# A four-layer graph kernel: T's row sums asked for one stage later, and layer 3's first group put through layer 2's pipeline

## The chip, the core and the metric

The kernel runs on one core of a Trainium2 chip. The metric is the device time of one launch in microseconds (us); less is better. The engines are TensorE (PE in the rows; its weight loads are PEld), VectorE (DVE), ScalarE (ACT), GpSimd (POOL) and SyncE (SP), which issues all DMAs. Each engine works through its own queue in order and waits at semaphores. Semaphores count up; `wait_ge(sem, n)` holds the queue until the count is n.

## What is computed

There are 128 graphs of 64 nodes with 512 features. Each of four layers adds an attention-like term to x. Cut to the parts that matter here:

```python
def gnn3(X, A):                                   # layer 3
    Xw = X @ Wv + bv
    sj, si = Xw @ aw[:d, 0], Xw @ aw[d:, 0]
    e = leaky_relu(sj[:, None, :] + si[:, :, None] + ab[0], 0.2)
    alpha = A * exp(e)
    T = alpha / (sum(alpha, axis=-1) + 1e-12)
    H, Xk = 0, X
    for k in range(3):
        H = H + Xk @ Wk[k] + bk[k]
        Xk = T @ Xk
    return relu(H)

# each layer, 0 to 3
h = maximum(layernorm(x), 0.0)
x = x + gnn_layer(h, adj)
```

Layer 2 is multi-head attention with 8 heads of 64, whose scores are multiplied by twice the adjacency ahead of the softmax, with projections q, k, v and o.

## The kernel before

All 8192 tokens are cut into 16 groups (`NG`) of 512 tokens, and each group into 4 tiles of 128 tokens (two graphs). A float32 product is made of three passes over values split in two parts, `hi` and `lo`: ScalarE copies the `hi` part and VectorE or GpSimd subtracts to get `lo`. Each engine's queue is written out by hand, one function for each (`pe_program`, `dve_program`, `act_program`, `pool_program`, `sp_program`), with the layers' loops over groups in it. Nothing reorders them.

Results of TensorE lie in 8 banks, taken in turn; each waits for the eviction of what lay there eight takes before. `bank.done(key)` is the wait for a bank's result.

The way of a group's input: SyncE loads x; VectorE makes statistics (`stats_A`, L629 and L631); GpSimd makes the scale (`scale_A`, L1188 to L1193); ScalarE normalizes into `hn` (`norm_A`, L961); VectorE transposes blocks into `hs` (`transposes`, L650); SyncE gathers `hs` into `hGA` with 16 DMAs (`gather`, L1392); ScalarE and another engine split this into `hi` and `lo` (`features2_hi`, L947, and `features_lo`, L1201).

Layer 2, group g. TensorE: q projection, first half of the context of group g-1 (`l2_ctx`), k projection, output tile 0 of g-1 (`l2_out`), second half of the context, output tiles 1 to 3 with the scores between, v projection, and the transposes of the probabilities P (`l2_pT`). ScalarE evicts these into `ptc` (L1139), and VectorE evicts v into `VV` (L877); the next context needs both. A further pass of the loop, g = NG, does what remains of the last group.

Layer 3, group g. TensorE makes z2 = h W2 in four tiles; then four tiles of z1 = h W1, each with the product of T and z2 added by three matmuls (a "hop", `l3_hop`, L589); then four tiles of y = h W0, each with the hop of T and z1. The hops need `T`'s parts (count `v_tlo`) and z's (`Z0`, `Z1`).

T of a group comes about like this. VectorE makes the sums `scol` over `hn` (`l3_sums`, L935, L940). SyncE writes one column to DRAM (L1425), waits, and reads it back spread over all partitions as `si` (L1429; `rows3`). VectorE adds and takes the leaky relu (`l3_alpha`, L817, L821), ScalarE the exponential (L1099), GpSimd multiplies with the adjacency, giving `al` (L1312). TensorE sums rows of `al` with a matrix of ones (`l3_rowsum`, L583). VectorE takes the reciprocal (L888, L890), GpSimd multiplies (`tt`, L1319), ScalarE and VectorE split the product into `T` (`Thi`, `Tlo`).

Before, all this for group g+1 is asked for within group g: the row-sum matmul stands behind y tile 1 of group g on TensorE, and the rest of T behind it on the others. And layer 3's group 0 has its own places in the last passes of layer 2: its statistics, norm and transposes stand between and behind the last group's softmax, and its weights `W3[2]` are split in the extra pass.

Of the kernel before, what the change touches and what calls it, by code (L numbers as in the profile page):

```python
# [74 lines left out]
def build(nc, x, adj, nodemask, L0_gnn_Wqk, L0_gnn_Wv, L1_gnn_Wq_w, L1_gnn_Wq_b, L1_gnn_Wk_w, L1_gnn_Wk_b,  # L75
# [12 lines left out]
    with root:  # L88
# [183 lines left out]
        def pe_program(eng):  # L272
# [266 lines left out]
            for g in range(NG + 1):  # L539
# [22 lines left out]
                for u in range(2):  # L562
# [3 lines left out]
                    if on:  # L566
                        l2_scores(g, u)
                if on:
# [7 lines left out]
            def l3_rowsum(g):  # L576
                if g >= NG:
                    return
# [13 lines left out]
            for g in range(NG):  # L592
# [14 lines left out]
                for t in range(4):  # L607
                    b, full, _ = gemm_open(("y", g, t), hT3[i], t, W3[0], (v_y, 4 * g + t + 1), False)
                    l3_hop(b, full, g, t, 1)
                    if t == 1:  # L610
                        l3_rowsum(g + 1)


        def dve_program(eng):
# [208 lines left out]
            for g in range(NG + 1):  # L823
# [6 lines left out]
                if g + 1 < NG:  # L830
                    stats_A(2, g + 1)
                if g == NG - 1:
                    dve.wait_ge(d_vec3, 64)
                    for k in range(4):
                        eng.scalar_tensor_tensor(sc3[:], wv3[:, k, :], 1.0, awb[:, 0, :], ALU.mult, ALU.mult,
                                                 accum_out=af[:, k, 0:1]).then_inc(v_af, 1)
                        dve.wait_ge(v_af, k + 1)
                if prev:
                    l2_out(g - 1, 0)
                if g + 1 < NG:  # L840
                    transposes(2, g + 1)
# [4 lines left out]
                if g == NG - 1:  # L846
                    for k in range(4):
                        eng.scalar_tensor_tensor(sc3[:], wv3[:, k, :], 1.0, awb[:, 1, :], ALU.mult, ALU.mult,
                                                 accum_out=af[:, k, 1:2]).then_inc(v_af, 1)
                        dve.wait_ge(v_af, k + 5)  # L850
# [3 lines left out]
                for u in range(2):  # L854
# [5 lines left out]
                    if u == 0 and g == NG - 1:  # L860
                        stats_A(3, 0)
                if g == NG - 1:
                    transposes(3, 0)
                    m = dve.step(eng.tensor_tensor(sc3[:], awb[:, 0, :], awb[:, 1, :], ALU.add))
                    dve.wait_ge(s_dve, m)
                    m = dve.step(eng.scalar_tensor_tensor(sc3[:], sc3[:], 1.0, bvb[:], ALU.mult, ALU.mult, accum_out=cst))
                    dve.wait_ge(s_dve, m)
                    eng.tensor_tensor(cst, cst, abc, ALU.add).then_inc(v_cst, 1)
# [13 lines left out]
            def l3_rowsum(g):  # L882
                if g >= NG:
                    return
# [5 lines left out]
                eng.reciprocal(rs[:], rs[:]).then_inc(v_rs, 1)  # L890
                dve.wait_ge(a_thi, 2 * g + 2)
# [7 lines left out]
            for g in range(NG):  # L899
                if g + 1 < NG:  # L900
                    stats_A(3, g + 1)
                for t in range(4):
                    l3_zlo(0, ("z2", g, t), g, t)
                    if g == 0 and t == 0:
                        l3_rowsum(0)
# [7 lines left out]
                l3_alpha(g + 1)  # L913
                xt = xs[x_slot(kA(3, g))]
                for t in range(4):
# [6 lines left out]
                    if t == 1:  # L922
                        l3_rowsum(g + 1)
# [19 lines left out]
        def act_program(eng):  # L943
# [157 lines left out]
            for g in range(NG + 1):  # L1101
# [11 lines left out]
                if g + 1 < NG:  # L1113
                    norm_A(2, g + 1)
# [9 lines left out]
                if g == NG - 1:  # L1124
                    norm_A(3, 0)
                if on:
                    l2_exp(g, 1)
                else:
                    split_in_place(W3[1], d_w1)
                if g + 1 < NG:  # L1130
                    act.wait_ge(*bank.done(("v2", g - 1, 3) if g else ("v1", NG - 1, 3)))
                    features2_hi(2, g + 1, hT2[(g + 1) % 2])
# [452 lines left out]
```

## Time and profile before

| | us |
|---|---|
| median of 3 runs | 2554.03 (2552.31 to 2554.06) |
| the profiled execution | 2550.87 |
| its span, first to last instruction | 2549.1 |
| TensorE busy, by the page | 2379.6 (93% of the span) |
| VectorE busy | 1357.8 (53%) |
| ScalarE busy | 818.2 (32%) |
| GpSimd busy | 816.5 (32%) |
| mean granted clock of TensorE | 0.968 of full speed |

The profile's page holds the busy time of each engine, the span cut into 40 slices, and the costliest groups of instructions. Behind it lie views that can be asked for: the timeline of one engine, who waited for whom, the DMA issues, and sums over stretches. A gap in square brackets is the idle time of the engine before the row, with what ended it. The layers take up, one after another, roughly 1200 us for layers 0 and 1, to 1730 us for layer 2, and the rest for layer 3. Instructions are pipelined, so on TensorE a row's start minus the start of the row before is its cost.

### The profile page before, as it was taken

The numbers are of one execution on the slowest core, as the hardware profiler recorded it, in microseconds if no ns is written. First come the engines' busy times: TensorE is split into PE (matmuls) and PEld (weight loads), VectorE is DVE, ScalarE is ACT, GpSimd is POOL, SyncE is SP. The second block draws the span as 40 slices with busy tenths as digits, with TensorE's granted clock in tenths as the row PEclk, the third lists the DMA queues.
The fourth block names the chain that finished last, engine by engine and source line by source line (L and its number), as shares of the span: only waits on it lengthen the run. The fifth ranks groups of instructions, "written<-read, shape, count | busy, mean of one in ns | idle before, by whom it ended". The sixth has DMA issues, their size and how long they took to land.

```text
span 2549.1 us, 39522 instructions
## 1 busy us (share of the span) xinstructions
PE 2379.6 (93%) x15951; PEld 1935.6 (76%) x15951; DVE 1357.8 (53%) x2570; ACT 818.2 (32%) x1493; POOL 816.5 (32%) x1015
## 2 busy tenths in 40 slices
PE   8899999999999999999999999997788878878887
PEld 4688888888888887888888888886677667766766
DVE  2565556656565545445444544556555555555553
ACT  2343334334343433333333333333112212221220
POOL 2354545545455333233223322325111111111120
PEclk9999999999999999999999999999899989988999
DMA  5223332233323432112212221234222223222320
GB/s 161 71 71 88 107 80 78 75 92 99 84 74 80 128 108 81 55 55 80 84 55 57 82 79 55 60 93 142 60 79 77 64 60 91 73 60 61 92 52 37
DMA packets 164007, 202.70 MB, mean 80 GB/s; under 512 B 71712, under 2 KB 71792, under 8 KB 163824
## 3 DMA queue, kind: packets, MB, share of 16 engines
q1 hardware_dynamic: 163824, 200.18, 27.8%
q8 instruction: 125, 2.05, 0.4%
q14 instruction: 58, 0.48, 0.1%
HBM read 82.62 MB, written 50.37 MB: 52 GB/s over the span
## 4 chain that ended last, share of the span: by engine, by line
PE 71%; issue 9%; SPq 6%; DVE 6%; ACT 3%; DMA 2%; POOL 2%; ACTq 0%; DVEq 0%; POOLq 0%
PE bank L313 32%; PE bank L303 27%; SPq L1392 6%; PE bank L329 2%; PE bank L375 2%; DVE hs L650 2%; ACT hn L961 1%; DVE stA L629 1%; PE bank L522 1%; ACT Z_hi L947 1%; PE bank L495 1%; DMA hGA<-hs 1%; PE bank L293 1%; PE bank L589 1%; PE bank L505 1%
## 5 line engine op out<-in xcount | busy, mean ns | idle before, releaser
L313 PE MATMUL bank<-w_hi,h3T_hi 128*128 128x512 f32 x768 | 317.6, 414 | 0.0
L313 PE MATMUL bank<-w_lo,h3T_hi 128*128 128x512 f32 x768 | 309.5, 403 | 0.0
L313 PE MATMUL bank<-w_hi,h3T_lo 128*128 128x512 f32 x768 | 308.4, 402 | 0.0
L961 ACT ACTIVATE hn<-x,stA 128x512 f32<-128x512 f32 x192 | 140.7, 805 | 168.8 <-POOL stA L1193 167.7
L313 PEld LDWEIGHTS bank<-w_hi,h3T_hi 128*128 128x128 f32 x768 | 152.1, 198 | 32.8
L313 PEld LDWEIGHTS bank<-w_lo,h3T_hi 128*128 128x128 f32 x768 | 151.4, 197 | 32.7
L313 PEld LDWEIGHTS bank<-w_hi,h3T_lo 128*128 128x128 f32 x768 | 150.6, 196 | 33.1
L1188 POOL TENSOR_SCALAR stA<-stA 128x4 f32<-128x4 f32 x48 | 11.6, 241 | 512.0 <-DVE stA L631 511.8
L618 DVE TENSOR_TENSOR Z_lo<-bank,Z_hi 128x512 fp32r<-128x512 f32 x128 | 81.4, 685 | 172.4 <-ACT Z_hi L947 172.4
L650 DVE STREAM_TRANSPOSE hs<-hn 128x512 f32<-128x512 f32 x192 | 123.7, 688 | 73.6 <-ACT hn L961 73.6
L1201 POOL TENSOR_TENSOR h3T_lo<-hGA,h3T_hi 128x512 fp32r<-128x512 f32 x64 | 84.5, 1322 | 228.8 <-ACT h3T_hi L947 228.8
L618 DVE TENSOR_TENSOR cT_lo<-bank,cT_hi 128x256 fp32r<-128x256 f32 x128 | 44.8, 410 | 205.2 <-ACT cT_hi L947 205.2
L629 DVE BATCH_NORM_STATS2 stA<-x 128x6 f32<-128x512 f32 x192 | 128.0, 666 | 7.4 <-DMA x<-in_x 7.4
L583 PE MATMUL bank<-alt,bones 128*128 128x256 f32 x32 | 19.0, 697 | 117.4 <-POOL alt L1312 117.4
L1239 POOL TENSOR_TENSOR vv_lo<-vf,vv_hi 128x512 fp32r<-128x512 f32 x64 | 82.6, 1290 | 115.7 <-ACT vv_hi L947 115.7
L303 PE MATMUL bank<-h0T_hi,m_hi 128*128 128x512 f32 x256 | 101.5, 397 | 14.4 <-POOL h0T_lo L1201 14.4
L1201 POOL TENSOR_TENSOR h0T_lo<-hGA,h0T_hi 128x512 fp32r<-128x512 f32 x64 | 99.7, 1588 | 38.9 <-ACT h0T_hi L947 38.9
L790 DVE TENSOR_TENSOR x<-bank,x 128x512 f32<-128x512 f32 x64 | 41.8, 675 | 131.2 <-PE bank L313 122.2
L1272 POOL TENSOR_TENSOR x<-x,abf 128x512 f32<-128x512 f32 x64 | 80.6, 1296 | 79.1 <-ACT hn L961 79.1
L313 PE MATMUL bank<-v_hi,h0T_hi 128*128 128x512 f32 x256 | 104.7, 409 | 0.0
L1260 POOL TENSOR_TENSOR zt<-zt,sm 128x512 f32<-128x512 f32 x64 | 66.9, 1045 | 116.7 <-DVE sm L804 116.7
L313 PE MATMUL bank<-o2w_hi,cT_hi 128*128 128x512 f32 x256 | 103.7, 405 | 0.6 <-DVE cT_lo L618 0.6
(235 smaller groups left out, 6204.0 us busy)
## 6 DMA issues: line engine op xcount, KB each, us to landing
hGA<-hs SPq DMA_DIRECT2D x768, 64.0 KB, 2.0
mid<-x SPq DMA_DIRECT2D x32, 1024.0 KB, 4.7
x<-mid SPq DMA_DIRECT2D x32, 1024.0 KB, 5.8
x<-in_x SPq DMA_DIRECT2D x16, 1024.0 KB, 6.0
hGB<-hs SPq DMA_DIRECT2D x256, 64.0 KB, 2.0
out<-x SPq DMA_DIRECT2D x16, 1024.0 KB, 4.9
abf<-in_adj SPq DMA_DIRECT2D x64, 64.0 KB, 5.0
adj<-in_adj SPq DMA_DIRECT2D x64, 64.0 KB, 3.4
```

Source lines behind the costliest of these rows:

```text
L303: ins = eng.matmul(b[:], W[l][:, k, os], h[r][:, k, :], start=(k == 0 and i == 0), stop=(k == 3 and i == 2))
L313: ins = eng.matmul(b[:], h[l][:, k, ts], W[r][:, k, :], start=(k == 0 and i == 0), stop=(last and k == 3 and i == 2))
L329: ins = eng.matmul(b[h, t * 64:(t + 1) * 64], left[:, k, ts], right[:, 2 * i:2 * i + 2, 4 * k + t, :], start=(k == 0), stop=(k == 3))
L618: return eng.tensor_tensor(lo, src, hi.bitcast(F), ALU.subtract)
L629: m = dve.step(eng.bn_stats(st[:, t, 0:6], xt[:, t, :]))
L650: eng.transpose(hs[:, :, :, t, :].rearrange("p b c r -> p c b r"), (hn1 if layer == 1 else hn)[t][:].rearrange("p (c b r) -> p c b r", c=4 ...
L961: eng.activation(h[t][:], xt[:, t, :], ACT.Relu, bias=st[:, t, 10:11], scale=st[:, t, 9:10]).then_inc(done, 1)
L1201: eng.tensor_tensor(by_token(h["lo"], q), hG[:, q], by_token(h["hi"], q).bitcast(F), ALU.subtract).then_inc(done, 1)
L1239: eng.tensor_tensor(vv["lo"][:, t, :], vf[t % 2][:], vv["hi"][:, t, :].bitcast(F), ALU.subtract).then_inc(p_vlo, 1)
L1260: eng.tensor_tensor(z3, z3, s8(sm[r][:, 0:8]), ALU.subtract).then_inc(p_sb, 1)
L1272: eng.tensor_tensor(xt[:, t, :], xt[:, t, :], bo2[:], ALU.add).then_inc(p_xb, 1)
L1392: eng.dma_start(hG[b * 32:b * 32 + 32, q].rearrange("p c r -> p (c r)"), hs[q * 32:q * 32 + 32, b].rearrange("p c t r -> p (c t r)")).then ...
```

## The change

No instruction's work is changed and none is added or left out of the computation; waits and places in the queues are.

In layer 3, `l3_rowsum(g)` moves from group g-1's y tile 1 to behind the first z2 tile of group g itself, on all engines. On VectorE it is cut in two: the reciprocal goes behind the first Z0 eviction and the split of T (`l3_tlo`) behind the second. `l3_alpha(g+1)` moves on VectorE from ahead of the y evictions to behind y tile 1.

Between layers 2 and 3, a helper `after2(g)` names the group that follows group g of layer 2: (2, g+1), or (3, 0) behind the last. Statistics, scale, norm, transposes and gather of (3, 0) take the place in the loop that such steps of a next group always have. The preparatory sums (`af`, `cst`), the zeroing of `abf`, and the split of `W3[2]` move with them. SyncE gathers ahead of loading `W3[2]` and `W3[1]`, which change places. The adjacency transpose of group 0 moves one output tile back on TensorE. In the diff below, the pieces up to line 610 are of TensorE, those from 827 to 922 of VectorE, from 1104 to 1171 of ScalarE, at 1328 of GpSimd and at 1508 of SyncE.

```diff
+        def after2(g):
+            return (2, g + 1) if g + 1 < NG else (3, 0)
...
@@ -553,7 +557,6 @@
                     l2_out(g - 1, 0)
-                    l3_adj(0)
...
+                    elif u == 0:
+                        l3_adj(0)
...
@@ -595,8 +598,8 @@
-                    if g == 0 and t == 0:
-                        l3_rowsum(0)
+                    if t == 0:
+                        l3_rowsum(g)
...
-                    if t == 1:
-                        l3_rowsum(g + 1)
...
@@ -827,27 +828,28 @@
-                if g + 1 < NG:
-                    stats_A(2, g + 1)
+                if on:
+                    stats_A(*after2(g))
                 if g == NG - 1:
                     dve.wait_ge(d_vec3, 64)
-                    for k in range(4):
...
+                    for h in range(2):
+                        for k in range(4):
...
+                    m = dve.step(eng.tensor_tensor(sc3[:], awb[:, 0, :], awb[:, 1, :], ALU.add))
...
+                if on:
+                    transposes(*after2(g))
...
-                    if u == 0 and g == NG - 1:
-                        stats_A(3, 0)
-                if g == NG - 1:
-                    transposes(3, 0)
...
@@ -901,8 +894,10 @@
+                    if t == 0:
+                        l3_rowsum(g)
+                    if t == 1:
+                        l3_tlo(g)
...
-                l3_alpha(g + 1)
                 xt = xs[x_slot(kA(3, g))]
...
                     if t == 1:
-                        l3_rowsum(g + 1)
+                        l3_alpha(g + 1)
...
@@ -1104,14 +1098,10 @@
-                if not on:
-                    split_in_place(W3[2], d_w2)
-                    act.wait_ge(v_cst, 1)
-                    features2_hi(3, 0, hT3[0])
...
+                elif on:
+                    act.wait_ge(v_cst, 1)
+                    features2_hi(3, 0, hT3[0])
+                    split_in_place(W3[2], d_w2)
...
@@ -1161,8 +1152,8 @@
+                    if t == 1:
+                        l3_thi(g)
...
-                l3_thi(g + 1)
...
@@ -1328,12 +1313,13 @@
+                if g:
+                    if g + 1 < NG:
+                        scale_A(3, g + 1)
+                    l3_rowsum(g)
...
-                l3_rowsum(g + 1)
...
@@ -1508,7 +1493,12 @@
-                gather(2, g + 1)
+                if on:
+                    gather(*after2(g))
+                if g == NG - 1:
+                    sp.wait_ge(*bank.done(("k2", g, 3)))
+                    eng.dma_start(W3[2]["raw"][:], rows(L3_gnn_Wk[2])).then_inc(d_w2, 16)
+                    eng.dma_start(W3[1]["raw"][:], rows(L3_gnn_Wk[1])).then_inc(d_w1, 16)
```

VectorE in layer 3, before, from the second y eviction of a group to the transposes for the next (`rst` the row sums, `yt` the y evictions, `BN_STATS` the statistics):

```order
L921 SCALAR_TENSOR_TENSOR x<-yt,x 128x512
L888 TENSOR_SCALAR rst<-bank 128x256
L890 RECIPROCAL rst<-rst 128x256
L618 TENSOR_TENSOR Tlo<-ttt,Thi 64x4x64 x2
L919 TENSOR_TENSOR yt<-bank,bsumt 128x512
L921 SCALAR_TENSOR_TENSOR x<-yt,x 128x512
L919 TENSOR_TENSOR yt<-bank,bsumt 128x512
L921 SCALAR_TENSOR_TENSOR x<-yt,x 128x512
L629 BN_STATS stA<-x 128x6
...
L618 TENSOR_TENSOR Z_lo<-bank,Z_hi 128x512 x2
L650 STREAM_TRANSPOSE hs<-hn 128x4x4x32 x4
```

VectorE in layer 3 with the change, from the end of alpha:

```order
L822 SCALAR_TENSOR_TENSOR ec<-zct 128x256
L913 TENSOR_TENSOR yt<-bank,bsumt 128x512
L915 SCALAR_TENSOR_TENSOR x<-yt,x 128x512
L913 TENSOR_TENSOR yt<-bank,bsumt 128x512
L915 SCALAR_TENSOR_TENSOR x<-yt,x 128x512
L630 BN_STATS stA<-x 128x6
...
L619 TENSOR_TENSOR Z_lo<-bank,Z_hi 128x512
L879 TENSOR_SCALAR rst<-bank 128x256
L881 RECIPROCAL rst<-rst 128x256
L619 TENSOR_TENSOR Z_lo<-bank,Z_hi 128x512
L619 TENSOR_TENSOR Tlo<-ttt,Thi 64x4x64 x2
L651 STREAM_TRANSPOSE hs<-hn 128x4x4x32 x4
```

The reciprocal and T's split have left the middle of the y evictions and stand between the Z evictions, behind the statistics; alpha (`zct`, `ec`) has gone into the y evictions.

ScalarE from layer 2 to layer 3, before (`zt` the exponentials of the softmax, `hn` the norm, `ptc` the transposed probabilities, `w_hi` the weights of layer 3, `cT_hi` the context):

```order
L1091 ACTIVATE zt<-zt 128x512 x2
L961 ACTIVATE hn<-x,stA 128x512 x4
L1091 ACTIVATE zt<-zt 128x512 x2
L947 ACTIVATE ptc<-bank 128x512 x4
L947 ACTIVATE cT_hi<-bank 128x4x64 x4
L947 ACTIVATE w_hi<-w_raw 128x512 x4
L947 ACTIVATE h3T_hi<-hGA 128x16x32 x4
L947 ACTIVATE cT_hi<-bank 128x4x64 x4
```

ScalarE there with the change:

```order
L1085 ACTIVATE zt<-zt 128x512 x4
L941 ACTIVATE h3T_hi<-hGA 128x16x32 x4
L941 ACTIVATE w_hi<-w_raw 128x512 x4
L941 ACTIVATE ptc<-bank 128x512 x4
L941 ACTIVATE cT_hi<-bank 128x4x64 x8
L941 ACTIVATE atc<-bank 64x256 x2
L1093 ACTIVATE ec<-ec 128x256
```

The norm of layer 3's group 0 has moved from between the exponentials to ahead of the context, and the `h3T_hi` and `w_hi` copies have moved from behind the context's first half to ahead of the `ptc` copies.

## Rows read from the trace of the kernel before

**Rows 1.** The page of the profile, its first line.
```profile
span 2549.1 us, 39522 instructions
```

**Rows 2.** Waits, 1769 to 2468 us: who <- for whom: us, times, longest.
```profile
PE bank L583 <- POOL alt L1312: 109.1, 14, 8.3
...
DVE yt L919 <- PE bank L589: 24.4, 17, 2.0
```

**Rows 3.** Timeline, TensorE: start us, us, line, tiles [idle before <-releaser].
```profile
1995.05 1.22 PE L583 MATMUL bank<-alt,bones 128*128 128x256 f32 x2 [7.93 <-POOL alt L1312]
...
2031.60 0.50 PE L589 MATMUL bank<-Z_hi,Thi 128*128 128x512 f32 x1
...
2504.55 0.39 PE L313 MATMUL bank<-w_hi,h3T_hi 128*128 128x512 f32 x1
...
2542.40 0.39 PE L589 MATMUL bank<-Z_hi,Tlo 128*128 128x512 f32 x1
```

**Rows 4.** Timeline row of TensorE, then busy times and granted clock of a stretch.
```profile
1783.10 0.79 PE L589 MATMUL bank<-Z_hi,Thi 128*128 128x512 f32 x1 [2.17 <-DVE Z_lo L618]
...
1783.07:1786.48 3.41, 3.38 (x8) 2.71 (x9) 1.76 (x3) 1.33 (x4) 0.11 (x1) 0.50 0.00 0
```

**Rows 5.** Timeline, SyncE's DMA issues in layer 3.
```profile
1769.00 3.10 SPq L1392 DMA_DIRECT2D hGA<-hs  x5
...
1969.31 10.06 SPq L1392 DMA_DIRECT2D hGA<-hs  x16
...
1987.82 0.34 SPq L1429 DMA_DIRECT2D sirows<-si  x1
...
2018.21 10.06 SPq L1392 DMA_DIRECT2D hGA<-hs  x16
...
2467.79 10.94 SPq L1392 DMA_DIRECT2D hGA<-hs  x16
```

**Rows 6.** Timeline, VectorE, one turn of layer 3.
```profile
1992.41 0.87 DVE L817 TENSOR_TENSOR zct<-sirows,stB 64x256 f32<-64x256 f32 x2 [7.97 <-DMA sirows<-si]
...
1996.79 0.42 DVE L888 TENSOR_SCALAR rst<-bank 128x256 f32<-128x256 f32 x1
...
2000.73 0.87 DVE L618 TENSOR_TENSOR Tlo<-ttt,Thi 64x256 fp32r<-64x256 f32 x2 [1.74 <-ACT Thi L947]
...
2005.40 0.69 DVE L629 BATCH_NORM_STATS2 stA<-x 128x6 f32<-128x512 f32 x1
...
2014.45 1.29 DVE L618 TENSOR_TENSOR Z_lo<-bank,Z_hi 128x512 fp32r<-128x512 f32 x2 [5.76 <-ACT Z_hi L947]
...
2015.65 2.48 DVE L650 STREAM_TRANSPOSE hs<-hn 128x512 f32<-128x512 f32 x4
```

**Rows 7.** Timeline, TensorE, from layer 2 to layer 3.
```profile
1731.56 3.69 PE L522 MATMUL bank<-ptc,VV 64*64 64x64 f32 x128 [6.99 <-DVE VV L877]
...
1742.26 1.11 PE L338 MATMUL bank<-ident,abf 128*128 128x128 f32 x4 [3.43 <-DMA abf<-in_adj]
...
1752.44 0.39 PE L313 MATMUL bank<-w_hi,h3T_hi 128*128 128x512 f32 x1
```

**Rows 8.** Timeline, VectorE's first reduction of L835, then SyncE.
```profile
1687.97 0.68 DVE L835 SCALAR_TENSOR_TENSOR sc<-wv,awb 128x512 f32<-128x512 f32 x1
...
1705.88 0.93 SPq L1504 DMA_DIRECT2D arows<-stB  x2
...
1714.52 0.33 SPq L1506 DMA_DIRECT2D arowt<-arows  x1
```

**Rows 9.** Timeline, ScalarE, from layer 2 to layer 3.
```profile
1723.20 2.07 ACT L947 ACTIVATE ptc<-bank 128x512 f32<-128x512 f32 x4 [1.97 <-PE bank L505]
...
1734.72 2.21 ACT L947 ACTIVATE w_hi<-w_raw 128x512 fp32r<-128x512 f32 x4
```

**Rows 10.** DMA issues near 1716.7 and 1735.7: KB each, us to landing.
```profile
w_raw<-in_L_gnn_Wk SPq DMA_DIRECT2D x1, 1024.0 KB, 9.0
...
w_raw<-in_L_gnn_Wk SPq DMA_DIRECT2D x1, 1024.0 KB, 5.9
```

More of the change, by code:

```diff
@@ L829, in dve_program @@
                     l01_x2(NG - 1, range(4))
-                if g + 1 < NG:
-                    stats_A(2, g + 1)
+                if on:
+                    stats_A(*after2(g))
                 if g == NG - 1:
                     dve.wait_ge(d_vec3, 64)
-                    for k in range(4):
-                        eng.scalar_tensor_tensor(sc3[:], wv3[:, k, :], 1.0, awb[:, 0, :], ALU.mult, ALU.mult,
-                                                 accum_out=af[:, k, 0:1]).then_inc(v_af, 1)
-                        dve.wait_ge(v_af, k + 1)
+                    for h in range(2):
+                        for k in range(4):
+                            eng.scalar_tensor_tensor(sc3[:], wv3[:, k, :], 1.0, awb[:, h, :], ALU.mult, ALU.mult,
+                                                     accum_out=af[:, k, h:h + 1]).then_inc(v_af, 1)
+                            dve.wait_ge(v_af, 4 * h + k + 1)
+                    m = dve.step(eng.tensor_tensor(sc3[:], awb[:, 0, :], awb[:, 1, :], ALU.add))
+                    dve.wait_ge(s_dve, m)
+                    m = dve.step(eng.scalar_tensor_tensor(sc3[:], sc3[:], 1.0, bvb[:], ALU.mult, ALU.mult, accum_out=cst))
+                    dve.wait_ge(s_dve, m)
+                    eng.tensor_tensor(cst, cst, abc, ALU.add).then_inc(v_cst, 1)
                 if prev:
                     l2_out(g - 1, 0)
-                if g + 1 < NG:
-                    transposes(2, g + 1)
+                if on:
+                    transposes(*after2(g))
                 if prev:
@@ L1163, in act_program @@
                     l3_zhi(0, ("z2", g, t), g, t)
-                    if g == 0 and t == 1:
-                        l3_thi(0)
+                    if t == 1:
+                        l3_thi(g)
                     if g == 0 and t == 3:
@@ L1276, in pool_program @@
                 on, prev = g < NG, g >= 1
-                if g + 1 < NG:
-                    scale_A(2, g + 1)
-                if g == NG:
-                    pool.wait_ge(v_vv, 4 * NG)
-                    pool.wait_ge(p_xb, 4 * NG)
-                    for tl in abf:
-                        eng.memset(tl[:], 0.0).then_inc(p_abz, 1)
+                if on:
+                    scale_A(*after2(g))
                 l2_residual(g + 1)
@@ L1287, in pool_program @@
                         l2_softmax(g, u)
-                    if u == 0 and g == NG - 1:
-                        scale_A(3, 0)
                 if g == NG - 1:
@@ L1299, in pool_program @@
                             eng.memset(tl[n][:].bitcast(F), 0.0).then_inc(p_zero3, 1)
-                if g == NG:
+                    pool.wait_ge(v_vv, 4 * NG)
+                    pool.wait_ge(p_xb, 4 * NG)
+                    for tl in abf:
+                        eng.memset(tl[:], 0.0).then_inc(p_abz, 1)
+                    features_lo(3, 0, hT3[0], hGA, p_flo3)
                     split_in_place(W3[2], "w2")
-                    features_lo(3, 0, hT3[0], hGA, p_flo3)
             def l3_alpha(g):
@@ L1330, in pool_program @@
             for g in range(NG):
-                if g and g + 1 < NG:
-                    scale_A(3, g + 1)
+                if g:
+                    if g + 1 < NG:
+                        scale_A(3, g + 1)
+                    l3_rowsum(g)
                 if g + 1 < NG:
@@ L1519, in sp_program @@
                 if g == NG - 1:
-                    sp.wait_ge(*bank.done(("qk", g, 2)))
-                    eng.dma_start(W3[1]["raw"][:], rows(L3_gnn_Wk[1])).then_inc(d_w1, 16)
-                    eng.dma_start(W3[2]["raw"][:], rows(L3_gnn_Wk[2])).then_inc(d_w2, 16)
-                    gather(3, 0)
                     sp.wait_ge(*bank.done(("pT", g, 3)))
```

30 lines of the change are left out of this document (5 added, 25 removed).

## The prediction, made before the changed kernel was run

> **What bounds the kernel now.** I read the page first: the span is 2549.1 us [rows 1], TensorE is busy over nine tenths of it, and the digits of the slices fall from 9 to 7 and 8 only in layer 3. So I listed who waits for whom between 1769 and 2468 us. TensorE sat idle 109.1 us, 14 times, before the matmul of L583 that sums T's rows, each time for `al` [rows 2]. VectorE waited 24.4 us for y's banks. TensorE's timeline shows one such wait: idle 7.93 us before 1995.05, then running [rows 3]. The idle costs clock too: a stretch of 3.41 us after a wait of 2.17 us was granted 0.50 [rows 4], which is 1.2 instead of 2.4 GHz.
>
> Why is `al` late? SyncE's queue and VectorE's timeline, read together, give a ring [rows 5, 6]. The gather for group g+1 starts at 1969.31; its 16 issues stand ahead of the store and reload of `si`; the reload is issued at 1987.82, and VectorE takes up the landed rows at 1992.41. Then come two y evictions, the row sums' reciprocal, T, two more y evictions, the next statistics (2005.40), the norm, two Z_lo, the transposes (2015.65), and the next gather (2018.21). Fourteen turns from 1769.00 to 2467.79 make 49.91 us each [rows 5]. A whole group's 168 matmuls in the last group, where nothing waits, take 2504.55 to 2542.79, 38.24 us, or 0.228 us each [rows 3]. **Layer 3 is bound by this ring of latencies, not by TensorE.** What counts is the steps that leave it.
>
> **Part 1, the row sums a stage later.** No work is added or removed. By the new VectorE order, y tiles 0 and 1 are evicted before the alpha step, in the time in which VectorE waited for `si`; tiles 2 and 3 follow alpha.
>
> Walk the new ring with the old durations, from a gather's start. Alpha starts after 23.1 us (1992.41 - 1969.31) [rows 5, 6]. To the statistics: 4.38 us (1996.79 - 1992.41), as before, since alpha and two evictions stand there again, now of tiles 2 and 3. Statistics, GpSimd's scale, ScalarE's norm and Z0_hi: 9.05 us (2014.45 - 2005.40). One Z_lo: 0.6 us (half of 2015.65 - 2014.45). Reciprocal, `tt`, T_hi, T_lo: 4.8 us (1996.79 to 2000.73 and 0.87 more). Transposes to gather: 2.56 us. The new stand of the row sums thus stays in the ring: in ScalarE's order the norm is ahead of Z0_hi, and VectorE takes the sums behind the first Z_lo. What leaves is (a) two evictions, 2.79 us, with the wait for y's banks, 24.4 / 14 = 1.74 us [rows 2], together 4.53 us, the mean from T_lo's end to the statistics; and (b) the second Z_lo, 0.6 us, now hidden under GpSimd's and ScalarE's part of T. The new turn is 49.91 - 5.13 = **44.8 us**. For fourteen turns: **-71.8 us**.
>
> Is `al` in time? It ended about 2.6 us after alpha's start (1995.05 - 1992.41) [rows 3, 6], so 25.7 us after the gather. z2(g+1) starts 24.4 us after the gather: the y0 hop at 13.4 (2031.60 - 2018.21), 0.8 for it, three tiles of 15 matmuls at 3.4. The sum is due 2.7 us after that, at 27.1. It waits for nothing, with 1.4 us to spare.
>
> **What is late next.** TensorE needs T at the first z1 tile, 60 matmuls and the sum after z2's start, 14.1 us. T is ready at 44.8 - 24.4 - 2.6 = 17.8. A new wait of 3.7 us appears at the hop (L589), for T_lo. Behind it in TensorE's queue stands everything; T_hi on ScalarE holds the Z0_hi of tiles 2 and 3 behind it, which TensorE needs 6 us later. The transposes come some 4 us later against z2 than now, so Z1_hi, queued behind the h3T copies on ScalarE, makes the y0 hop wait as well: 31.9 asked, 20.4 + 13.4 = 33.8 ready, 1.9 us. Work 39.1, waits 5.6: again 44.7. Both waits are slack of TensorE, not additions to the ring: y3 is ready at 24.4 and its eviction starts at about 26.
>
> The clock, by rows: half speed for 3.41 us after a wait of 2.17 us [rows 4] loses 1.7 us. After the wait for T this only shortens the second wait. So I take 0, up to +0.6 us a turn (+8) if 10 us at half speed follow it, as y3 would then be 0.6 us late. The Trainium skill, TensorE: Matmul & The Clock Gate, "HAM oscillation — how this bites in real kernels", speaks against the change: short work between waits pays the return to speed at every wait, and two waits now stand where one was. By that rule alone a turn would cost what a second slow stretch costs; the ring's slack hides it by the rows.
>
> **Part 2, the change from layer 2 to 3.** Before, TensorE waits 6.99 us (to 1731.56, for V) and 3.43 us (to 1742.26, for the adjacency of group 0) and starts z2(0) at 1752.44 [rows 7]. V is late since the statistics, the transposes and the work on `cst` of layer 3 stand between and behind layer 2's last softmax on VectorE. They move ahead, into 9 us in which VectorE was idle: 3.3 us of statistics and eight reductions at 0.73 (four start at 1687.97 [rows 8]) end near 1697.2, 8.7 us before the 1705.88 at which SyncE sends their result. Two more operations on `cst` end by 1698.8, before out(14,0) asks at 1699.8. These cost nothing under that cover.
>
> SyncE: everything behind these reductions moves by 8.7 us. The row reload goes from 1714.52 to 1705.8 [rows 8]; the gather of layer 3 follows at once, 16 issues in 10.7 us, to 1716.8; then W3[2] is loaded, now first of the three large transfers. VectorE's V is done near 1723.4, right behind the last v2 tile. **But ScalarE's queue now has W3[2]'s four copies (2.21 us) ahead of the four copies of P^T (2.07 us)** [rows 9], and these wait for the weights. A 1 MB load landed in 9.0 us as first of two behind a store, in 5.9 us alone [rows 10]. I take 5.9, since it has no large transfer ahead of it any more: landed 1722.8, split 1725.0, P^T 1727.1. TensorE resumes at 1727.1 instead of 1731.56, -4.45. With 9.0 us it is 1730.1, -1.4; as the last of three large ones (some 12 us) even +1.5.
>
> The fixed cost and rate in the Trainium skill, DMA: Bandwidth & Descriptors, "Anatomy of one DMA — SWDGE (gpsimd) path", would make it an estimate of 4.4 us; P^T would then wait for TensorE's last transpose instead, and the sum would change by under 1 us.
>
> The 3.43 us go: the zeroing of the diagonal buffers moves behind V on GpSimd, 7 us earlier, and the adjacency transpose moves one output tile back. Alpha(0) gets its `si` some 11 us earlier too (an estimate: V is 7.9 us earlier, and the gather's issues, which hold SyncE's next loads some 4 us beyond the zeroing now, stand ahead of it), and its sum is due only after z2(0)'s first tile, near 1747. Group 0 then runs as now, bound by TensorE to its z2 tiles. Sum of part 2: **-4.45 - 3.43 = -7.9 us**, between -12 and -2.
>
> **The tail.** Now 81.3 us pass from the last gather (2467.79) to the end. Then: 24.4 to z2(15), 38.24 + 0.4 for its matmuls and sum with no wait (no statistics stand ahead of its row sums), 6.3 from the last matmul to the end (2549.1 - 2542.79): 69.4. **-11.9 us.**
>
> **Sum:** -7.9 - 71.8 - 11.9 = -91.6 us. The profiled execution took 2550.87 us, so 2459.3; against the median of 2554.03, 0.1% above it, **2462 us**.
>
> **Rivals.**
> 1. T is in time and TensorE alone bounds layer 3: a turn of 39.1 us, 14 x -10.8 = -151, in all -171, **2383 us**. For it: the waits for `al` are all that TensorE shows now. Against: T's own steps and the 9.05 us of statistics and norm ahead of them are in the rows. 5%.
> 2. The ring is longer than its parts: y3, or the reload of `si`, comes later, because TensorE runs at half speed after both waits (rows of up to 10 us after 8 us of idle exist). With 10.2 and 6.8 us slow, y3 is ready near 31, 4 us late: a turn of about 48.8, **2518 us**; with one of them 2470. 12% beyond 2490.
> 3. W3[2] lands late and P^T with it, the last term from +1.5: about **2468 us**, inside the range. 8%.
> 4. Slower: TensorE does not return to 2.4 GHz between waits 14 and 30 us apart. At half speed throughout, 168 matmuls take 77 us, a turn of 78: +390, **2940 us**. It decides from a turn of 49.91 + (7.9 + 11.9) / 14 = 51.3 us, that is 24 us of each group at half speed; now it is 7 to 10. The skill's clock page reports a clock stuck low for over 50 us, a case of this kind; no row here shows it. 2%.
> 5. The change does not do what it says: `al` is still late and the old wait returns at the new place. The margin is 1.4 us, and reloads vary by 1 us. But a late sum has 9 us until VectorE asks for it, so the turn stays: same time. Held in the forecast.
>
> **Chances.** Forecast 73%, rival 1 5%, 2 12%, 3 8%, 4 2%. The range 2440 to 2490 holds the forecast (turn of 43.5 to 46.5) and rival 3. A measurement of this kernel can tell 0.2%, 5 us, from no change. Faster 96%, the same 1%, slower 3%.
>
> **What would show it.** After: the wait before the row-sum matmul gone; 14 waits of 2 to 4 us of the hop for T_lo, and some of 1 to 2 us for Z1_lo; gathers 44.8 us apart, the first near 1761; P^T's copies starting at 1725 on ScalarE, behind the weights; no wait for the adjacency. Gathers 39 us apart prove rival 1, over 47 rival 2. A first gather later than 1767 makes part 2 wrong.

## The result, and the profile after

The changed kernel took **2462.16 us** (median of 4 runs, 2460.24 to 2465.29), the kernel before 2553.53 us beside it (2552.31 to 2554.06). The ratio is **0.9644**, 95% interval 0.9627 to 0.9661: 3.6% faster. The forecast was 2462 us, faster.

| | before | after | early_sums (below) |
|---|---|---|---|
| span of the profiled execution, us | 2549.1 | 2459.3 | 2379.8 |
| gather for layer 3's group 1 starts at | 1769.00 | 1760.75 | 1762.33 |
| gather for the last group starts at | 2467.79 | 2388.72 | 2306.52 |
| one turn (difference / 14) | 49.91 | 44.86 | 38.87 |
| from the last gather to the end | 81.3 | 70.6 | 73.3 |
| mean granted clock | 0.968 | 0.986 | 0.994 |

Of the 89.8 us by which the span is shorter, 8.25 lie ahead of the first gather, 70.8 in the 14 turns (5.06 each), and 10.7 behind the last gather.

The page's first line and its TensorE line (busy us, share of the span, instructions):

```profile
span 2459.3 us, 39508 instructions
...
PE 2364.3 (96%) x15951; PEld 1923.9 (78%) x15951; DVE 1360.9 (55%) x2570; ACT 820.3 (33%) x1493; POOL 818.1 (33%) x1015
```

Waits of the changed kernel from 1769 to 2389 us (who, for whom: us in total, times, longest), which answer to [rows 2]:

```profile
DVE zct L818 <- DMA sirows<-si: 50.8, 14, 4.2
...
PE bank L592 <- DVE Tlo L619: 43.5, 14, 3.6
DVE yt L913 <- PE bank L592: 22.2, 15, 3.0
...
PE bank L592 <- DVE Z_lo L619: 10.6, 6, 2.3
```

TensorE's 109.1 us for `al` are gone from the list. In their place stand 14 waits for T_lo and 6 for Z_lo, 54.1 us together.

One turn, which answers to [rows 5, 6]. SyncE, with a gather, the reload of `si` and the next gather:

```profile
1806.25 10.28 SPq L1377 DMA_DIRECT2D hGA<-hs  x16
1816.57 0.58 SPq L1410 DMA_DIRECT2D si<-stB  x1
1826.01 0.33 SPq L1414 DMA_DIRECT2D sirows<-si  x1
...
1850.99 10.06 SPq L1377 DMA_DIRECT2D hGA<-hs  x16
```

VectorE in the same turn:

```profile
1829.57 0.87 DVE L818 TENSOR_TENSOR zct<-sirows,stB 64x256 f32<-64x256 f32 x2 [3.86 <-DMA sirows<-si]
...
1833.95 0.69 DVE L630 BATCH_NORM_STATS2 stA<-x 128x6 f32<-128x512 f32 x1
...
1842.99 0.69 DVE L619 TENSOR_TENSOR Z_lo<-bank,Z_hi 128x512 fp32r<-128x512 f32 x1 [5.75 <-ACT Z_hi L941]
1843.60 0.41 DVE L879 TENSOR_SCALAR rst<-bank 128x256 f32<-128x256 f32 x1
...
1848.43 2.49 DVE L651 STREAM_TRANSPOSE hs<-hn 128x512 f32<-128x512 f32 x4
```

And TensorE and GpSimd there: `al`, its row sums, and the hop that waits for T_lo:

```profile
1831.43 0.73 POOL L1298 TENSOR_TENSOR alt<-ec,atc 128x256 f32<-128x256 f32 x1 [11.46 <-ACT ec L1093]
...
1833.62 0.59 PE L586 MATMUL bank<-alt,bones 128*128 128x256 f32 x2
...
1848.45 0.80 PE L592 MATMUL bank<-Z_hi,Thi 128*128 128x512 f32 x1 [3.31 <-DVE Tlo L619]
```

Each step of this turn, with the forecast in brackets: gather to alpha 23.32 us (forecast 23.1), alpha to statistics 4.38 (4.38), to the first Z_lo 9.04 (9.05), the Z_lo 0.61 (0.6), reciprocal to T_lo's end 4.83 (4.8), transposes to the next gather 2.56 (2.56): 44.74 us. `al` ends at 1832.16, 1.46 us before the matmul that needs it (forecast 1.4), and no turn has a wait for it. Only group 0's `al`, in the passage, came 0.57 us late (1747.29).

TensorE from layer 2 to layer 3 in the changed kernel, which answers to [rows 7]:

```profile
1728.91 2.10 PE L526 MATMUL bank<-ptc,VV 64*64 64x64 f32 x128 [2.92 <-ACT ptc L941]
...
1732.34 0.50 PE L317 MATMUL bank<-o2w_hi,cT_hi 128*128 128x512 f32 x1 [1.33 <-DVE cT_lo L619]
...
1737.91 0.60 PE L342 MATMUL bank<-ident,abf 128*128 128x128 f32 x4
...
1743.84 0.39 PE L317 MATMUL bank<-w_hi,h3T_hi 128*128 128x512 f32 x1
```

z2(0) starts 8.60 us earlier (1752.44 to 1743.84), near the 7.9 of the forecast, but by other terms. The next rows show it. They cover both kernels from TensorE's return to z2(0). Each row has the length in us and TensorE's busy time (instructions). Then come the same for the weight loads, VectorE, ScalarE and GpSimd, and the granted clock, the DMA share and GB/s. Of before:

```profile
1731.56:1742.26 10.70, 6.72 (x141) 5.68 (x141) 5.95 (x18) 6.45 (x16) 7.60 (x8) 0.82 0.65 168
1742.26:1752.44 10.18, 10.18 (x41) 8.49 (x41) 0.00 (x0) 0.76 (x2) 3.14 (x3) 0.84 0.12 27
```

Of the changed kernel:

```profile
1728.91:1738.20 9.29, 7.96 (x155) 6.81 (x156) 5.26 (x12) 2.42 (x8) 7.97 (x7) 1.00 0.68 192
1738.20:1743.84 5.64, 5.64 (x27) 4.66 (x26) 0.00 (x0) 0.76 (x2) 0.00 (x0) 1.00 0.21 39
```

TensorE came back 2.65 us earlier, not 4.45. The 3.43 us for the adjacency went, as forecast. A wait for cT_lo (the `lo` part of the context) grew from 0.56 to 1.33 us, which I had not counted; TensorE had run the context ahead of it in 2.10 instead of 3.69 us and so asked sooner. And TensorE was busy 13.60 instead of 16.90 us, since the clock stayed at full speed (1.00) where it had fallen to 0.82 and 0.84: 3.30 us that I had taken as 0. Sum: -2.65 - 3.43 + 0.77 - 3.30 = -8.61.

This sum is of one execution. In another of the same kernel (after_again, below) z2(0) started at 1748.23, 4.4 us later, with a longer wait for cT_lo and the clock at 0.83 from 1725 to 1745 us:

```profile
1733.85 0.80 PE L317 MATMUL bank<-o2w_hi,cT_hi 128*128 128x512 f32 x1 [2.71 <-DVE cT_lo L619]
...
1748.23 0.39 PE L317 MATMUL bank<-w_hi,h3T_hi 128*128 128x512 f32 x1
```

### The profile page after: what moved, and what is told of

Same layout as the page of the kernel before. It is cut to its first block, busy times and chain, and to the rows that moved or that the text cites. A ratio compares the mean times of both kernels' runs of the same rounds, so it can differ in the third digit from the quotient of the medians.

```text
span 2459.3 us, 39508 instructions
## 1 busy us (share of the span) xinstructions
PE 2364.3 (96%) x15951; PEld 1923.9 (78%) x15951; DVE 1360.9 (55%) x2570; ACT 820.3 (33%) x1493; POOL 818.1 (33%) x1015
## 4 chain that ended last, share of the span: by engine, by line
PE 69%; DMA 8%; DVE 8%; SPq 6%; issue 3%; ACT 3%; POOL 2%; ACTq 0%; DVEq 0%; POOLq 0%
PE bank L317 30%; PE bank L307 28%; SPq L1377 6%; DMA si<-stB 5%; PE bank L333 3%; DMA sirows<-si 3%; PE bank L379 2%; DVE hs L651 2%; DVE stA L630 1%; ACT hn L955 1%; PE bank L499 1%; PE bank L526 1%; PE bank L297 1%; DVE rst L881 1%; PE bank L509 1%
## 5 line engine op out<-in xcount | busy, mean ns | idle before, releaser
L317 PE MATMUL bank<-w_hi,h3T_hi 128*128 128x512 f32 x768 | 311.1, 405 | 0.0
L317 PEld LDWEIGHTS bank<-w_hi,h3T_lo 128*128 128x128 f32 x768 | 148.2, 193 | 32.4
L619 DVE TENSOR_TENSOR cT_lo<-bank,cT_hi 128x256 fp32r<-128x256 f32 x128 | 44.8, 411 | 204.0 <-ACT cT_hi L941 204.0
L592 PE MATMUL bank<-Z_hi,Thi 128*128 128x512 f32 x128 | 54.1, 423 | 55.4 <-DVE Tlo L619 43.5
L929 DVE SCALAR_TENSOR_TENSOR yt<-hn,arowt 128x512 f32<-128x512 f32 x128 | 102.1, 852 | 0.0
```

What stands on the lines that cost most here:

```text
L317: ins = eng.matmul(b[:], h[l][:, k, ts], W[r][:, k, :], start=(k == 0 and i == 0), stop=(last and k == 3 and i == 2))
L619: return eng.tensor_tensor(lo, src, hi.bitcast(F), ALU.subtract)
L929: eng.scalar_tensor_tensor(yt[c][:], hn[t][:], 0.0, arow[:, c, :], ALU.max, ALU.mult, accum_out=scol[g % 2][:, t, c:c + 1]).then_inc(v_dot ...
```

## Experiments: the two parts alone

The theory: layer 3 runs at the length of a ring of latencies from gather to gather, part 1 takes 5.1 us out of each turn, part 2 is a one-time gain, and TensorE's new waits are slack. The first rival is that TensorE's waits or its clock set the turn; the second, that the parts' gains are shared out otherwise.

**part1_only**: only layer 3's new places, with the passage as before. Edit against the changed kernel, in short:

```diff
-                if on:
-                    gather(*after2(g))
+                gather(2, g + 1)
...
-                if on:
-                    stats_A(*after2(g))
+                if g + 1 < NG:
+                    stats_A(2, g + 1)
...
```

> Only the layer 3 part of the change: the row sums asked for in the group that needs T, alpha between the y evictions. The passage from layer 2 to 3 is that of the kernel before. Theory (a ring of latencies of 44.8 us a turn, independent of the passage): fourteen turns of 44.8 instead of 49.9 us and a tail 11 us shorter, together about -82 us, 2472 us, ratio 0.968; first gather for group 1 at about 1769 us. Rival (the two parts need each other, since a late group 0 keeps TensorE behind): less than -70 us, with turns above 46 us.

Measured: 2476.3 us (2474.6 to 2479.1), ratio 0.9683 (0.9667 to 0.9699), with the kernel before at 2558.15 us on that chip. Gathers from 1771.37 to 2405.48, a turn of 45.29; 14 waits for T_lo, 52.0 us. Part 1 alone brings 81.9 us.

**part2_only**: only the passage; layer 3's row sums and alpha as before. Edit against the changed kernel:

```diff
-                    if t == 0:
-                        l3_rowsum(g)
+                    if g == 0 and t == 0:
+                        l3_rowsum(0)
...
+                    if t == 1:
+                        l3_rowsum(g + 1)
```

> Only the passage: group 0 of layer 3 goes through layer 2's pipeline, and layer 3's loop is that of the kernel before. Theory: the first gather for group 1 comes 8 us earlier, turns stay at 49.9 us, so about -8 us, 2545 us, ratio 0.9968. Rival (a gain ahead of a loop bound by latencies is taken back by the loop's first wait): within 2 us of the kernel before.

Measured: 2548.16 us (2545.06 to 2549.1), ratio 0.9962 (0.9947 to 0.9977): 10.0 us, a small gain, but clear of the interval. The turn is 50.26 us, with this wait in layer 3 (1762 to 2465 us):

```profile
PE bank L588 <- POOL alt L1304: 113.7, 14, 8.4
```

The parts add up: 81.9 + 10.0 = 91.9 us, where the whole change brought 91.4 and, in after_again, 90.5. The wait for `al` belongs to part 1 and the gain in the passage to part 2.

## Experiments: what sets the turn

**after_again**: the changed kernel, as the base of this set.

> The changed kernel once more, for comparison on this chip: ratio 0.9644 to the kernel before.

Measured: 2467.01 us (2465.35 to 2469.24), ratio 0.9642 (0.9625 to 0.9659), before at 2557.48; a turn of 45.09.

**more_matmul**: the row-sum matmul is done five times, each with the same result: 1.4 us more for TensorE in each group.

```diff
-                eng.matmul(b[:, 0:256], bones[:], ...).then_inc(full, 1)
+                for i in range(5):
+                    ins = eng.matmul(b[:, 0:256], bones[:], ...)
+                ins.then_inc(full, 1)
```

> The changed kernel with the row-sum matmul of each group of layer 3 done five times into the same bank instead of once: four more, at 0.35 us each by the trace, are 1.4 us more work for TensorE in each of 16 groups. Theory (the turn is the ring of latencies, and the wait for T_lo is slack of TensorE): no change, within 4 us of the changed kernel, and the waits for T_lo shrink from about 3.1 to about 1.7 us. Rival (TensorE with its clock bounds the turn, and the ring only fits by chance): 16 times 1.4, +22 us, turns of 46.3 us.

Measured: 2469.88 us (2468.07 to 2470.42), ratio 0.9657 (0.9642 to 0.9671). It ran in the set of part1_only and not in that of after_again, so the ratios are compared: 0.0015 apart, 3.8 us, with intervals that overlap. Were TensorE the bound, 16 groups would have cost 22 us. TensorE's waits from 1765 to 2400 us took it up:

```profile
PE bank L594 <- DVE Tlo L621: 24.8, 14, 2.0
...
PE bank L594 <- DVE Z_lo L621: 16.9, 11, 1.9
```

The waits for T_lo have shrunk from 3.1 to 1.8 us each; the turn is 45.12 us, as it was. Not all of the added work shows in the waits: in this window they sum to 41.7 us, against 54.9 in after_again, and the mean granted clock was 0.991 against 0.982, so fewer slow stretches paid for part of it. But TensorE still waits for over 40 us, so it is not the bound.

**recip_twice**: VectorE takes one reciprocal more, into a scratch tile, in the ring between the row sums and T. **recip_in_gap**: the same reciprocal, but ahead of alpha, where VectorE waits for `si`. Both edits add this:

```diff
+                m = dve.step(eng.reciprocal(zc[:], rs[:]))
+                dve.wait_ge(s_dve, m)
```

> The changed kernel with the reciprocal of the row sums (1.75 us on VectorE) made twice in each group, the first time into a tile that nobody reads. It stands between the first Z eviction and T. Theory (this place is in the ring): every turn 1.8 us longer, 46.6 us, +26 us in all; ratio about 0.975. Rival (VectorE is busy for little over half of the time and absorbs it): within 5 us of the changed kernel.

> The changed kernel with the same additional reciprocal of 1.75 us per group on VectorE, but ahead of alpha, in the time in which VectorE waits for the rows of si (3.6 us a group by the trace). Theory: the work is hidden there, no change within 4 us. Rival (VectorE's load as such, or its contention, counts): the same +26 us as at the other place.

VectorE in recip_twice, with the two reciprocals in the ring:

```profile
1801.34 0.41 DVE L879 TENSOR_SCALAR rst<-bank 128x256 f32<-128x256 f32 x1
1801.79 1.75 DVE L881 RECIPROCAL zct<-rst 128x256 f32<-128x256 f32 x1
1803.58 1.75 DVE L883 RECIPROCAL rst<-rst 128x256 f32<-128x256 f32 x1
```

VectorE in recip_in_gap: the added one ends 2.3 us before alpha.

```profile
1827.09 1.75 DVE L917 RECIPROCAL zct<-rst 128x256 f32<-128x256 f32 x1
1831.13 0.88 DVE L818 TENSOR_TENSOR zct<-sirows,stB 64x256 f32<-64x256 f32 x2 [2.30 <-issue]
```

Measured: 2493.79 us in the ring (2493.13 to 2494.03), ratio 0.9746 (0.973 to 0.9762), a turn of 47.10; 2467.89 us in the gap (2466.33 to 2468.67), ratio 0.9644 (0.9625 to 0.9664). The same instruction costs **26.8 us in one place and 0.9 in the other**. By the traces the span grew by 26.2 us: the turns by 2.02 us each, 28.3 in all (1.79 is the added step itself, the rest stays open), with a first gather 1.6 us earlier and a tail 0.5 us shorter. So the place between the row sums and T is in the ring, and the one ahead of alpha is not. These two places alone are tested; the other members are read off the timeline, and the next run bears on them.

**early_sums**: on VectorE, the row sums, the transposes of the next group and T_lo now stand ahead of the Z_lo copies, and on ScalarE T_hi ahead of Z_hi. If the ring is the bound, this takes time out of it: the row sums and T no longer wait behind the norm and the copies of Z.

```diff
+                if g:
+                    l3_rowsum(g)
+                    if g + 1 < NG:
+                        transposes(3, g + 1)
+                    l3_tlo(g)
                 for t in range(4):
                     l3_zlo(0, ("z2", g, t), g, t)
-                    if t == 0:
+                    if g == 0 and t == 0:
                         l3_rowsum(g)
...
+                if g:
+                    l3_thi(g)
                 for t in range(4):
                     l3_zhi(0, ("z2", g, t), g, t)
```

> The changed kernel with VectorE taking the row sums' reciprocal of group g directly behind the statistics of group g+1, then the transposes, then T's split, and only then the first Z eviction; ScalarE copies T_hi ahead of Z0_hi. Theory: the reciprocal and T's steps then run beside GpSimd's scale and ScalarE's norm instead of behind them, the ring is some 36 to 37 us long, below TensorE's 39.1 us of work; turns of 39 to 40 us and no wait for T_lo: about -79 us against the changed kernel, 2383 us, ratio 0.933 to the kernel before. Rival (the ring's length lies in SyncE's gather, store and reload, and VectorE's order only shifts waits): turns stay above 43 us, at most -20 us.

Measured: **2382.39 us** (2381.63 to 2382.99), ratio **0.9315** (0.9302 to 0.9329). It beats both kernels. SyncE's gathers in the steady part are 39.02 us apart:

```profile
2228.44 11.25 SPq L1385 DMA_DIRECT2D hGA<-hs  x16
...
2248.44 0.34 SPq L1422 DMA_DIRECT2D sirows<-si  x1
...
2267.46 10.06 SPq L1385 DMA_DIRECT2D hGA<-hs  x16
```

From 1800 to 2300 us TensorE is busy without a gap, at full clock:

```profile
1800.00:2300.00 500.00, 500.00 (x2230) 413.48 (x2229) 349.91 (x670) 144.50 (x269) 113.50 (x125) 1.00 0.33 90
```

This is the time and the turn of rival 1, reached by an order that the changed kernel does not have. It shows what the changed kernel left: some 6 us a turn (44.86 and 45.09 us against 38.87), up to where TensorE is the bound. How much of it the earlier transposes bring, and how much the earlier T, no run tells apart.

## Experiments: what sets the passage

The forecast put P^T, held by W3[2]'s four copies ahead of it on ScalarE, on the path. Two theories were left: the weights' landing sets when z2(0) starts, or VectorE does.

**early_pt_first**: early_sums with the four weight copies behind P^T's.

```diff
                     features2_hi(3, 0, hT3[0])
-                    split_in_place(W3[2], d_w2)
                 if on:
...
+                if g == NG - 1:
+                    split_in_place(W3[2], d_w2)
```

> The kernel with the early row sums, and on ScalarE the four copies of W3[2] behind the copies of P^T instead of ahead. Theory: TensorE's wait for P^T on the passage goes, but the next wait, for the context's lower parts on VectorE, takes its place, as VectorE's last row products are stretched by GpSimd's work at the same time: within 2 us of the kernel with the early row sums (ratio 0.9315). Rival (P^T alone holds the passage): 1 to 2 us faster for each us that P^T comes earlier, at most 3 us; slower only if W3[2] is late for z2.

Measured: 2381.06 us (2380.36 to 2383.25), ratio 0.9307 (0.9291 to 0.9323), against 0.9315: no difference that these runs can tell. TensorE waited 0.94 us for P^T and 3.05 for cT_lo. But the same two waits were 0.94 and 3.04 us in early_sums: there the weights had come in time (their copies started at 1722.52), and P^T's copies followed TensorE's transposes in both kernels. TensorE in early_sums:

```profile
1726.91 2.10 PE L526 MATMUL bank<-ptc,VV 64*64 64x64 f32 x128 [0.94 <-ACT ptc L947]
1732.04 0.80 PE L317 MATMUL bank<-o2w_hi,cT_hi 128*128 128x512 f32 x1 [3.04 <-DVE cT_lo L619]
```

So this run took nothing off the path, and it does not decide between the theories. In the changed kernel the two waits were 2.92 and 1.33, in after_again 1.26 and 2.71, in part2_only 2.12 and 1.74: their sum was 3.9 to 4.3 us in these executions while the parts changed.

VectorE in the changed kernel, with slow row products:

```profile
1724.89 0.68 DVE L929 SCALAR_TENSOR_TENSOR yt<-hn,arowt 128x512 f32<-128x512 f32 x1
...
1726.11 1.75 DVE L929 SCALAR_TENSOR_TENSOR yt<-hn,arowt 128x512 f32<-128x512 f32 x1
...
1727.79 1.74 DVE L929 SCALAR_TENSOR_TENSOR yt<-hn,arowt 128x512 f32<-128x512 f32 x1
...
1729.57 1.12 DVE L934 TENSOR_SCALAR stB<-stB,small 128x4 f32<-128x4 f32 x1
1730.87 1.41 DVE L619 TENSOR_TENSOR cT_lo<-bank,cT_hi 128x256 fp32r<-128x256 f32 x4 [0.18 <-ACT cT_hi L941]
```

And GpSimd beside it:

```profile
1725.03 0.99 POOL L1286 MEMSET abf<- 128x512 f32 x2 [2.72 <-DVE VV L870]
1725.99 5.91 POOL L1191 TENSOR_TENSOR h3T_lo<-hGA,h3T_hi 128x512 fp32r<-128x512 f32 x4
```

The row product takes 0.68 us beside the memset and 1.75 beside h3T_lo. In this execution that cost cT_lo nothing, as it still waited 0.18 us for ScalarE; in early_sums and after_again cT_lo followed the products without a gap. The next run asks whether GpSimd is the cause.

**gpsimd_waits**: early_sums, with GpSimd waiting for the end of these products before it makes h3T_lo.

```diff
+                    pool.wait_ge(v_sc, 1)
                     features_lo(3, 0, hT3[0], hGA, p_flo3)
```

> early_sums with one wait more: GpSimd starts h3T_lo of layer 3's group 0 only when VectorE has finished the row products of that group. No work is added or removed. Collision theory (in the passage VectorE's last products take 1.75 us instead of 0.69 because GpSimd runs at the same time, and cT_lo is late for that): all products take 0.69 us, TensorE's wait for cT_lo in the passage falls from 3.0 to 1.4 us or less, about 2 us; the rest of the passage is as before unless w_lo of W3[2], now 2.6 us later on GpSimd, is late for z2(0), where up to 1 us is given back. Time 2380 to 2381 us against 2382 for early_sums. Rival (the 1.75 us are the products' own, or another cause): the last products stay at 1.75 us, cT_lo is no earlier, and the time stays or grows by the delay of w_lo.

**tile3_behind**: early_sums, with the products of token tile 3 behind cT_lo on VectorE.

```diff
                 if prev:
                     l2_ctx(g - 1, 0)
+                    if not on:
+                        l3_sums(dve, eng, 0, (3,))
...
-                            l3_sums(dve, eng, 0, ((0,), (1,), (2, 3))[t - 1])
+                            l3_sums(dve, eng, 0, ((0,), (1,), (2,))[t - 1])
```

> early_sums with the row products of token tile 3 of layer 3's group 0 moved behind cT_lo of the first half of the last context on VectorE. Theory (VectorE's queue, not the landing of W3[2] or P^T, holds the passage): ptc still waited for by about 0.9 us, the wait for cT_lo falls from 3.0 to 0.6 us or less, TensorE reaches the last output tiles 2.4 us earlier; cT_lo itself may be slowed by GpSimd's h3T_lo beside it. si leaves about 1.5 us later, which its slack before the row-sum matmul of group 0 covers or not: up to 1 us given back there. Time about 2380 us. Rival (the passage is held by weights or P^T): TensorE's wait returns elsewhere and z2(0) starts where it did.

**early_base**: early_sums again, as their base.

> The kernel of early_sums once more, as the base for the two others on the same chip: 2382 us, within 2; TensorE waits about 3.0 us for cT_lo in the passage; 39 us from gather to gather in layer 3.

VectorE in gpsimd_waits, the same two products and the operation behind them:

```profile
1727.72 0.69 DVE L935 SCALAR_TENSOR_TENSOR yt<-hn,arowt 128x512 f32<-128x512 f32 x1
...
1728.33 0.69 DVE L935 SCALAR_TENSOR_TENSOR yt<-hn,arowt 128x512 f32<-128x512 f32 x1
...
1729.06 0.23 DVE L940 TENSOR_SCALAR stB<-stB,small 128x4 f32<-128x4 f32 x1
```

1.75 has become 0.69 and 1.12 has become 0.23: that GpSimd's subtraction slows them is shown. GpSimd's h3T_lo itself took 4.96 instead of 5.92 us. The Trainium skill, SBUF — State Buffer, "SBUF: two separate sides", describes such a case: VectorE and GpSimd share a pair of ports, which goes to one of them for a whole instruction, and a VectorE operation with two inputs in SBUF is subject to it when the GpSimd operation reads SBUF. The trace of the products agrees, down to the memset, which reads nothing and slows nothing. That it is the ports is the skill's account; no run here separates them from another cause beside GpSimd. Why the 128x4 operation slowed as well, no run here asks.

But the time did not follow. gpsimd_waits took 2380.93 us (2378.15 to 2381.97), ratio 0.9302 (0.9288 to 0.9316); early_base 2380.5 (2379.1 to 2382.22), ratio 0.9302 (0.9289 to 0.9316). TensorE in early_base:

```profile
1729.29 3.63 PE L526 MATMUL bank<-ptc,VV 64*64 64x64 f32 x128 [2.17 <-ACT ptc L947]
1733.55 0.50 PE L317 MATMUL bank<-o2w_hi,cT_hi 128*128 128x512 f32 x1 [0.62 <-DVE cT_lo L619]
```

TensorE in gpsimd_waits:

```profile
1730.41 2.10 PE L526 MATMUL bank<-ptc,VV 64*64 64x64 f32 x128 [2.81 <-ACT ptc L947]
1733.84 0.50 PE L317 MATMUL bank<-o2w_hi,cT_hi 128*128 128x512 f32 x1 [1.33 <-DVE cT_lo L619]
```

I had expected early_base to wait 3.0 us for cT_lo and it waited 0.62: in this set W3[2] was issued at 1719.48 instead of 1716.72, P^T came later with it, and VectorE's products had time. TensorE also ran the context in 3.63 instead of 2.10 us, at a granted clock of 0.53, and so asked for cT_lo 1.5 us later. By the timelines the weights held early_base, gpsimd_waits and the changed kernel's first execution, and the products held early_sums, early_pt_first and after_again; the two lie close together. No run took the later of the two away in an execution that it held, so how much either costs in time is not shown. The 1.33 us in gpsimd_waits, with VectorE idle for 3.07 us before its cT_lo, is what the copies of the context by ScalarE and then VectorE cost TensorE once P^T is the last to come. The changed kernel's 1.33 us is the same.

tile3_behind took 2387.19 us (2384.76 to 2388.58), ratio 0.9325 (0.9309 to 0.9342), 6.7 us slower than early_base, where I had expected about 2380. TensorE's wait there:

```profile
1754.17 1.22 PE L586 MATMUL bank<-alt,bones 128*128 128x256 f32 x2 [5.31 <-POOL alt L1308]
```

The products started at 1733.76 behind cT_lo and took 1.79 and 1.77 us beside GpSimd's w_lo; `si` left at 1738.46 instead of 1731.86, 6.6 us later and not the 1.5 that I had counted. In early_base `al` of group 0 ended 0.4 us before its matmul (1747.42 and 1747.82). Here it ended 6.7 us later (1754.12), TensorE asked for it 1.0 us later, and the rest is the wait of 5.31. So the passage has no room for a later `si`: the margin is 0.4 us in early_base, and in the changed kernel `al` was 0.57 us late.

## Why the prediction was right

**The turn: right, in mechanism and size.** 44.86 us against 44.8, with every segment within 0.3 us. This rested on one choice: to follow the order from gather to gather with the old durations, instead of subtracting TensorE's wait of 7.8 us (109.1 / 14). The latter gives a turn of 42.1 and, with the other terms as they are, a time of about 2425. recip_twice and recip_in_gap show it for one place each: the one in the ring counts in full, the one beside it not at all.

**What is late next: right.** T_lo by 3.1 us on average (43.5 / 14, forecast 3.7), up to 3.6. Z_lo by 1.8, but in 6 of 14 turns only. `al` in time by 1.46 us. more_matmul shows that the waits are slack: they shrank, and the turn stayed.

**The clock in the turns: right to leave it out.** Behind a wait of 3.31 us the clock fell to 0.50, which is 1.2 instead of 2.4 GHz, for 6.83 us:

```profile
1847.27:1854.10 6.83, 5.65 (x13) 4.51 (x14) 6.51 (x16) 1.31 (x3) 0.00 (x0) 0.50 0.12 29
```

From 1720 us to the end of the span there are 12 such stretches with 48.8 us in the changed kernel, against 19 with 148.2 us before. Ten of the 12 stand at a wait for T_lo, 41 to 44 us after a gather, and run at most 4 us into the next turn, long before y3 (24.4); of the 14 waits for T_lo the four shortest, 1.81 to 2.72 us, have none. One stands at a wait of 2.03 us for Z_lo in the first turn (45.50 us), and the last at the end of the span. The rule of the Trainium skill that the prediction weighed (TensorE: Matmul & The Clock Gate, "HAM oscillation — how this bites in real kernels"), that every wait pays for a return to speed, holds here for 11 of the 20 waits in the turns; rival 4, slower, had nothing to stand on. The turns on both sides of the stretch above, 44.74 and 44.69 us, are no longer than the mean.

**The passage: the sum right in part by luck, its terms wrong.** -8.6 for a forecast of -7.9. The first step that failed was "P^T 1727.1": the gather's issues took 12.36 us instead of 10.7 and ended at 1718.83, so W3[2] was issued 2.1 us later; it landed within 5.8 us, as taken (the estimate of 4.4 us beside it was not met). P^T came at 1728.9. In early_sums, where the issues took 10.73 us, TensorE resumed at 1726.91, as forecast. The second step was the wait for cT_lo, taken as unchanged: it is 0.77 us longer. VectorE's row products were also taken at 0.69 us each although GpSimd's h3T_lo was moved beside them by the same change; the kernel before has rows of 1.8 us for such a pair in layer 3. In this execution they did not delay cT_lo, but in after_again they did. Their sum was ready at 1730.69, when SyncE had been free since 1729.17, so they held `si`. Alpha of group 0 then started 8.0 us earlier than before (1752.63 to 1744.64) and not some 11, and `al` was 0.57 us late. And I left out the clock, which gave 3.3 us back. early_sums and after_again had a slow stretch of 6.8 us in the same place, so this gain is not there in every execution: with z2(0) at 1748.23, after_again has 4.2 of the 8.6 us.

**The tail: 1.2 us short.** 70.6 against 69.4. z2 of the last group started 25.56 us after the gather (2388.72 to 2414.28) and not 24.4, since y's hop before it came at 14.54 us instead of 13.4; the rest, 45.0 us, was as counted (44.9).

Span against span, -89.8 us came of the -91.6 forecast. The turns missed by +1.0 us in all and the tail by +1.2; the first gather came 0.35 us earlier than forecast, but only since +1.8 for P^T and +0.8 for cT_lo in the passage met -3.3 for the clock. That the time came out at 2462.16 us for a forecast of 2462 is luck beyond the 2 or 3 us to which the terms were right.

**Rivals.** 1: a turn of 39.1 us was not the changed kernel's, but the bound named there is real: early_sums stands on it. 2 and 4: no row for them. 3: P^T was late, as there, by 1.8 us, and the clock paid for it.

## What to carry to other kernels

When a wait is large, look for the closed loop through the engines and DMAs behind it, and add up its segments with the durations of the trace; what a change brings is what leaves the loop, not the wait. An instruction added once inside the loop and once beside it (here 26.8 against 0.9 us) shows whether these two places belong to it, and then every step in the loop that need not stand ahead of the next can be moved out: four reordered calls brought another 3.4%. When a step moves to another place in a queue, look at which engine now runs beside it, too.

## What was not expected of the hardware

- A VectorE product of two tiles in SBUF, 0.69 us alone, took 1.75 us beside a GpSimd subtraction that reads SBUF, and 0.68 us beside a GpSimd memset. A small VectorE operation (128x4) went from 0.23 to 1.12 us beside the same subtraction. GpSimd's four subtractions took 4.96 us without and 5.91 us with the products beside them.
- One and the same kernel differs between sets of runs and between executions by more than early_pt_first and gpsimd_waits moved the time (1.3 and 0.4 us): the kernel before took 2553.53, 2558.15, 2557.48 and 2557.18 us in four sets of runs, the wait for cT_lo in one and the same kernel was 3.04 us (early_sums) and 0.62 us (early_base), and z2(0) of the changed kernel started at 1743.84 and at 1748.23.
- The 16 issues of one gather took SyncE 10.06 to 12.36 us within one trace, and the `si` column, 2 KB, needed 7.9 to 10.4 us in layer 3 of the changed kernel from its issue until the reload could be issued.
